# Attention over 16 images: a third buffer for stacked queries and keys, row maxima spread one to a slot, a shorter normalisation chain

## What is computed

```python
xn = (xg - mean) * rsqrt(var + EPS)          # 8 groups of 16 channels, per image
qkv = einsum('oc,bcn->bon', qkv_w, xn) + qkv_b
attn = softmax(einsum('bhdn,bhdm->bhnm', q * scale, k * scale))   # 8 heads, d = 16, n = m = 1024
out = einsum('bhnm,bhdm->bhdn', attn, v)
out = einsum('oc,bcn->bon', proj_w, out) + proj_b + x_in
```

## Time and profile before

| | us |
|---|---|
| median of the 3 runs | 5554.0 (5553.28 to 5566.23) |
| span of the profiled execution | 5548.6 |
| first exponential of image 0, start | 93.0 |
| last exponential of image 15, start | 2121.7 |
| first convolution matmul, start | 2172.2 |
| TensorE busy over the span | 4842.2 (87%) |
| VectorE busy over the span | 3586.2 (65%) |
| ScalarE busy over the span | 2987.7 (54%) |
| GpSimd busy over the span | 1021.9 (18%) |

### The profile page before, as it was taken

One profiled execution on the slowest core, in us unless ns is written; L12 is line 12 of the kernel. 1 busy time (PEld: TensorE's weight loads), 2 busy tenths in 40 slices (PEclk: granted clock), 3 DMA queues, 4 the chain that ended last, 5 costly groups with the idle time before them and its releaser, 6 DMA issues.

```text
span 5548.6 us, 81822 instructions
## 1 busy us (share of the span) xinstructions
PE 4842.2 (87%) x25633; PEld 2616.5 (47%) x25633; DVE 3586.2 (65%) x7699; ACT 2987.7 (54%) x5420; POOL 1021.9 (18%) x1348
## 2 busy tenths in 40 slices
PE   5888888888888886957888888888899999999999
PEld 1222222222222221336777877787755555555554
DVE  6677777777777762555665656555576676766765
ACT  2655565665655653414555555556755455455552
POOL 2212112121222112202333333333210000000000
PEclk7999999999999998979999999999999999999999
DMA  2522222222222211223545454544321111111112
GB/s 84 144 70 81 81 70 70 70 73 78 73 89 82 66 45 38 29 68 106 165 140 163 141 162 147 157 146 129 106 61 45 50 48 45 50 46 47 52 45 75
DMA packets 406297, 477.10 MB, mean 86 GB/s; under 512 B 87640, under 2 KB 249648, under 8 KB 403760
## 3 DMA queue, kind: packets, MB, share of 16 engines
q1 hardware_dynamic: 372128, 424.84, 25.4%
q0 software_dynamic: 20576, 35.55, 2.3%
q10 hardware_dynamic: 13168, 11.48, 0.8%
HBM read 308.54 MB, written 145.57 MB: 82 GB/s over the span
## 4 chain that ended last, share of the span: by engine, by line
PE 33%; DVE 15%; issue 3%; DVEq 3%; ACT 2%; ACTq 0%; SPq 0%; DMA 0%
PE n_ps_f L2153 4%; PE n_ps_f L2146 4%; PE n_ps_xy L1801 3%; PE n_ps_h L1791 3%; PE n_ps_c L2193 2%; PE n_ps_h L2205 2%; PE n_ps_f L2140 2%; PE n_ps_f L1649 2%; PE n_ps_xy L2209 1%; DVEq L2025 1%; DVE n_stats L971 1%; DVE n_xln L983 1%; PE n_ps_f L995 1%; PE n_ps_h L2209 1%; DVE n_down_weights L2024 1%
## 5 line engine op out<-in xcount | busy, mean ns | idle before, releaser
L597 ACT ACTIVATE a_probs<-ps_b 128x512 f32<-128x512 f32 x2048 | 1111.0, 594 | 794.8 <-PE ps_b L693 782.0
L454 DVE TENSOR_REDUCE a_negmax<-ps_a 128x1 f32<-128x1024 f32 x1024 | 1206.1, 1219 | 378.9 <-PE ps_a L637 369.3
L637 PE MATMUL ps_a<-a_k_stack,a_q_stack 96*128 96x512 bf16 x2048 | 634.6, 396 | 178.8 <-DVE a_negmax L454 89.9
L693 PE MATMUL ps_b<-a_q_stack,a_k_stack 99*128 99x512 bf16 x2048 | 673.6, 391 | 68.2 <-ACT a_probs L597 30.9
L1604 ACT ACTIVATE n_hidden<-n_ps_h,n_b 128x128 f32<-128x128 f32 x1472 | 420.2, 374 | 339.1 <-PE n_ps_h L1791 338.3
L706 PE MATMUL ps_o<-a_probs,a_v_ones 128*32 128x512 f32 x4096 | 562.0, 622 | 0.2 <-ACT a_probs L597 0.2
L637 PEld LDWEIGHTS ps_a<-a_k_stack,a_q_stack 96*128 96x128 bf16 x2048 | 146.1, 99 | 732.2 <-DVE a_negmax L454 468.9
L1801 PE MATMUL n_ps_xy<-n_down_weights,n_hidden 128*128 x2944 | 410.7, 284 | 78.9 <-ACT n_xy L1618 72.8
L693 PEld LDWEIGHTS ps_b<-a_q_stack,a_k_stack 99*128 99x128 bf16 x2048 | 196.2, 100 | 487.8 <-ACT a_probs L597 251.5
L1801 PEld LDWEIGHTS n_ps_xy<-n_down_weights,n_hidden 128*128 128x128 f32 x2944 | 369.1, 196 | 117.0 <-issue 112.8
L1791 PE MATMUL n_ps_h<-n_xy,n_up_weights 128*128 128x128 f32 x2944 | 399.8, 279 | 3.6 <-issue 1.8
(11 more groups left out here) (346 smaller groups left out, 7532.8 us busy)
## 6 DMA issues: line engine op xcount, KB each, us to landing
n_up_weights<-in_L_ffn_W_dram SPq DMA_DIRECT2D x368, 256.0 KB, 2.7
n_up_weights<-score_scratch SPq DMA_DIRECT2D x512, 128.0 KB, 2.9
split_scratch<-a_pieces SPq DMA_DIRECT2D x180, 256.0 KB
a_q_stack<-split_scratch SPq DMA_DIRECT2D x128, 192.0 KB, 3.7
a_k_stack<-split_scratch SPq DMA_DIRECT2D x128, 192.0 KB, 4.1
rows_scratch<-n_zero SPq DMA_DIRECT2D x16, 1472.0 KB, 10.5
outs_scratch<-n_xy SPq DMA_DIRECT2D x176, 128.0 KB, 1.9
n_xg<-rows_scratch SPq DMA_DIRECT2D x80, 256.0 KB
```

The lines of the kernel that those rows point to most:

```text
L454: dve.tensor_reduce(negmax[:, b, t:t + 1], bank, axis=AX.X, op=ALU.max, negate=True).then_inc(ring_read, 1)
L597: act.activation(probs[:, m % PROBS, 512 * k:512 * k + 512], ps_b[:, k, :], ACT.Exp).then_inc(b_exp, 1)
L637: last = pe.matmul(bank[:, cols], q_stack[0:KS, h, 128 * t:128 * t + 128], k_stack[0:KS, h, cols], start=True, stop=True)
L693: pe.matmul(ps_b[:, k, :], k_stack[:, h, 128 * t:128 * t + 128], q_stack[:, h, 512 * k:512 * k + 512], start=True, stop=True).then_inc(b_u ...
```

## The change

- A third stack buffer, laid over the part of `u_cols` that images 12 to 15 will fill at the end (`third`). Buffers are taken in turn by group (`stacks`). Results of images 12 and 13 go to DRAM first (`held_dram`) and are loaded when the last image runs (`load_held`).
- Of the six products four are stored instead of six, since two slots repeat (`STORED`); a stack is loaded as three DMAs of 32 rows by four heads for queries and three for keys (`PAIRED`), and TensorE waits once per group for all six.
- Each slot has one R, four slots ahead of where it stood by group (`LEAD`), 32 in 32 slots.
- Order on TensorE: in even slots the first ring unit, S, W, then the other ring units; in odd slots S, then the ring units. W is in every even slot.
- The normalisation chain is shorter (two operations per Newton step instead of three, fewer for the variance and the shift) and is cut into pieces that stand in slots of their own, as are the moments, `norm2` and `turn2`.
- `normed` has the query product in slot 10, the key product in 12, values in 14 (4, 6 and 9 before). Query, key, value and projection products are whole pairs of matmuls, as they were.
- GpSimd does the first shift of the second group before `divide`.

```diff
-        PRODUCTS = ((0, 0), (0, 1), (1, 0), (1, 1), (0, 2), (2, 0))
+        PRODUCTS = ((0, 0), (1, 1), (1, 0), (0, 1), (0, 2), (2, 0))
+        STORED = ((0, 1, 0, 2), (0, 1, 2, 0))
+        PAIRED = ((0, 1, 2), (0, 0, 2))
+        BUFFERS = 3
+        LEAD = 4
+        HOLD = B - 4
+        third = u_cols[:, HOLD:B, :, :].rearrange("p a c h -> p (a c h)").bitcast(BF16).rearrange("p (s j n) -> p s j n", s=2, j=J)
...
-            work = [(0, ("moments",)), (1, ("sums", 0)), (1, ("norm",))]
-            return work + [(4, ("qk", 0)), (6, ("qk", 1)), (9, ("v",))]
+            work = [(0, ("stats", 0, 0)), (1, ("stats", 0, 1)), (2, ("moments", 0)), (3, ("sums", 0))]
+            work += [(4, ("affine", 0, 0)), (6, ("affine", 0, 1)), (8, ("affine", 0, 2)), (9, ("norm",))]
+            return work + [(10, ("qk", 0)), (12, ("qk", 1)), (14, ("v",))]
...
-            return [(2, ("take", 1)), (8, ("recip",)), (29, ("project",)), (30, ("moments2",)),
-                    (31, ("sums", 1)), (32, ("norm2",)), (34, ("turn2",))]
+            work = [(3, ("take", 1)), (8, ("recip",)), (30, ("project",)), (31, ("stats", 1, 0)), (33, ("stats", 1, 1)), (35, ("moments", 1))]
+            work += [(36, ("sums", 1)), (37, ("affine", 1, 0)), (39, ("affine", 1, 1)), (41, ("affine", 1, 2))]
+            work += [(43, ("norm2", 0)), (45, ("norm2", 1))]
+            return work + [(47 + 2 * k, ("turn2", k)) for k in range(4)]
...
-            work = [(3 + n * 26 // QUAD, ("scores", ahead, g, n)) for n in range(QUAD)]
-            return work + [(18, ("shift", ahead, g, 0)), (30, ("shift", ahead, g, 1))]
+            work = [(n, ("scores", ahead, g, n)) for n in range(QUAD)]
+            return work + [(17, ("shift", ahead, g, 0)), (33, ("shift", ahead, g, 1))]
...
+            def load_stacks(i, g):
+                if G * i + g >= BUFFERS:
+                    sp.wait_ge(b_up, (G * i + g - BUFFERS + 1) * (2 * QUAD))
+                for qk, stack in enumerate(stacks(i, g)):
+                    sp.wait_ge(split_stored[qk], (i + 1) * SPLIT)
+                    for n, slot in enumerate(PAIRED[qk]):
+                        sp.dma_start(stack[2 * D * n:2 * D * n + 2 * D, :, :],
+                                     split_dram[qk, J * g:J * g + J, slot:slot + 2, :, :].rearrange("j s d n -> (s d) j n")).then_inc(stacked(i, g)[0], 16)
...
-                    n = run(works, kind, i, n, table)
+                    units_of_slot = [work for work in works if work[0] in RING]
+                    if m % 2:
+                        shifted_scores(i, m)
+                        n = run(units_of_slot, kind, i, n, table)
+                        continue
+                    n = run(units_of_slot[:1], kind, i, n, table)
                     shifted_scores(i, m)
-                    if m % J < HALVES:
-                        if m >= J:
-                            weigh_values(i, m // J - 1, m % J)
-                        elif kind != "first":
-                            weigh_values(i - 1, G * NT - 1, m % J)
+                    if m >= J:
+                        weigh_values(i, m // J - 1, m % J // 2)
+                    elif kind != "first":
+                        weigh_values(i - 1, G * NT - 1, m % J // 2)
+                    n = run(units_of_slot[1:], kind, i, n, table)
```

195 lines of the change are left out of this document (110 added, 85 removed).

## The result

The changed kernel took 5484.5 us (median of 4 runs, 5470.64 to 5493.7), the kernel before 5556.3 on the same chip (5553.28 to 5566.23). The ratio is 0.9868, its 95% interval 0.985 to 0.9886: **72 us or 1.3% faster**. Forecast were 5438 us and 116 us less, with a range of 5315 to 5525. The profiled execution is the fastest of the four, 14 us under the median: 5470.64 us, span 5468.8, which is 79.8 under the span of before.

A forecast was written before the change was run, and what follows sets the result against it. TensorE was taken to bound it, with a floor of 101.3 us an image; 18.7 of waits made 120.0, 7.6 less. Fourteen images gave 106, the prologue 11, the last image lost 1: 116 less, 5438 us, range 5315 to 5525.

The forecast's parts named there:

- the four slots' 0.87: Wait per four slots holding plain scores (R) in the kernel before, 11 us over 52 slots; the new order removes it.
- (a): Query and key product, slots 10 and 12: shifted scores (S) wait for ScalarE's product reading and exponentials, 6.5 us an image.
- (g): One stretch at the lower clock per image: a third of 4 us, 1.3 us.
- Rival C: Clock falls to 1.2 GHz and stays from slot 0 to 16: 16 us more per image, 5663 us; chance 0.07.
- (b): Value product's bank is read as long as that of plain scores (R); the second R behind waits 0.7 us.
- (f): Second halves of shifted scores (S) and turns of maxima: 1.2 us an image.
- (c): VectorE's statistics, chain and normalisation in slots 0 to 9 exceed its free time; TensorE waits about 3.9 us.
- (d): VectorE's work from slot 30 on (projection read, second chain, norm2, turn2) exceeds its free time: 3.0 us an image.
- (e): ScalarE's reading of the sums and copies of values delay exponentials: 2.1 us an image.
- rival D: Stack comes late: slow query and key loads make R in slot 28 wait some 7.5 us, 5545 us; chance 0.07.
- Rival B: Waits hide nearly all, only product waits and a little clock stay: 109.5 us an image, 5291 us; chance 0.16.
- E: Rival that the kernel does not do what it says; dismissed by the order on TensorE, no chance given.

The follow-up runs named there:

- run 3: The changed kernel with the order inside a slot as in the kernel before (all units, S, then W): 5498.1 us, ratio 0.9885 to before.
- run 10: Changed kernel with exponentials before product readings, first chain an image early, products and projection earlier, but the old order inside a slot: 5389.8 us, ratio 0.9685 to before.
- run 12: Changed kernel with exponentials before product readings, early first chain, earlier products, VectorE's work spread evenly, but the old order inside a slot: 5394.3 us, ratio 0.9708 to before.
- run 1: The changed kernel with ScalarE taking a slot's exponentials before reading the query or key product, first piece rounded later: 5482.5 us, ratio 0.9853 to before.
- run 6: The changed kernel with scratch laid out piece by piece: stores of 128 rows, six loads of 16 rows by 4 heads for three: 5483.9 us, ratio 0.9868 to before.

## Why the prediction came out as it did

It was right in sign and range, and 46 us too low in the median; by the two profiles 36 us of the forecast's 116 were missed. That is a balance of larger misses: the thirteen images fell 27 us short and the prologue 16, 5 more were missed behind the attention's images (7 in the part whose code is the same, less 2 won in the last image), and the image without a next one gave back 12. That these 12 stand against the rest is luck: the forecast had this image equal to the others.

**Order of R, S and W.** The pair came at 2.89 us (forecast 2.84), 1.5 us an image more. That "the four slots' 0.87 goes" holds: 0.6 per four slots in run 3, with one R a slot. What the step did not see is that the time so freed is for the most part taken by waits elsewhere in the image: undone, the order costs some 10 to 14 us of the whole (run 3, by ratio and by median, where the intervals overlap), nothing (run 10), or 11 us by median (run 12).

**(a) and (g), the products.** S lost 2.36, 0.82 and 2.38 us, 5.6 with its second halves, against the forecast's 6.5: right in size and place, and run 1 took it away. (g), "one stretch at the lower clock per image", was mis-sized: 1.3 forecast, and 2.8 measured, as R, S, W and the value product from 991 to 998 us took 0.4, 0.5, 0.9 and 1.1 longer. Rival C had the place right and not the size: the dip follows the two waits, but the clock comes back, and the 1.5 us over the forecast are a tenth of its price (16 us an image). Over the span the mean granted clock was 0.949 against 0.952. The Trainium skill, "TensorE: Matmul & The Clock Gate", section on a second failure mode, says that small idle times between groups of matmuls can make the clock swing between its two levels; the trace agrees with the swing at this place, and the rule alone gives no price.

**(b) to (f).** The value product's wait was 0.45 (0.7). (c) came to 3.2 (the waits at the group sum, 1.05 and 0.69, and 1.41 before the product) against 3.9. From slot 30 on, (d) and (e) together lost 5.6 against 5.1. So an image with a next one should have taken 120.0 and took 122.6: 1.5 of it for (g), 1.5 for the pairs, less what (a) to (c) came in under. These terms are read in an image of 121.7 us with a mean clock of 0.97; the other 0.9 of the mean go with images that have more time at 1.2 GHz (0.945 in four of the thirteen).

**The fourteen images** were taken as equal. The one without a next image gained 19.5 us, not 7.6; the thirteen gained 5.5.

**The prologue** was forecast as 11 us less and came 4.9 more; here the step failed, not a size. "Eight at 204 GB/s bring the stacks some 6 us earlier" had the rate of the stores too high: eight of 256 KB, since now both groups go out ahead, moved 143 to 180 GB/s, not 204. And it left out the loads. The first key load of a stack went out 2.7 us earlier (SyncE's queue, before and then changed):

```profile
49.26 0.43 SPq L286 DMA_DIRECT2D a_k_stack<-split_scratch  x1
```

```profile
46.55 1.25 SPq L317 DMA_DIRECT2D a_k_stack<-split_scratch  x3
```

But R now waits for a whole group, 5.5 us from there, where it waited 2.8 for one head. The first R stayed at 52.03. And "four R more are done ahead, which saves waits in image 0" left out what they cost where they stand: in a loop that goes at VectorE's pace and at half clock, these four, from 92.37 on, and slot 0's own R put the first S from 92.38 to 98.00.

**The third buffer.** "This cover is 6 us thick" was the thinnest place of the argument. The way took 38.0 us in run 1, not 32; forecast were 5.1 and 4.5 for stores and loads, and 9.5 and 6.8 came. TensorE took 39.8 us for these slots (976.83 to R of slot 28, the second pair of the row at 1016.24, which starts at 1016.7), not 38, and the waits (a) and the clock (g) are part of that. So 1.8 us were left, and rival D was that near. Rival B would have run into the stacks, as run 1 did: run 1 hides most of the waits at the products, leaves the stacks where they are, and takes 5482.5 us, not 5291. E fell with the trace.

## What to carry to other kernels

Before taking a wait away, follow the next chain that ends at the same place, and price it without the wait: here 7.4 us of waits hid a stack path with 1.8 us to spare, and nearly all of it came back. When a loop gets a cheaper order but other engines and a transfer are close behind, expect the saving back as waits for these; a side chain that is shorter and in pieces, and an even table, were worth more here (8.6 and 9.5 us an image) than the order (1.3). And price all transfers of a prologue up to the first use, the loads behind the stores too, at a rate measured for their size and layout.

## What the chip showed that was not expected

A store whose DRAM side is 8 heads by 16 rows kept the DMA engines at a share of 0.50 and moved 143 to 180 GB/s; the same bytes as 128 rows had 1.05 and 405 GB/s. The Trainium skill, "DMA: Bandwidth & Descriptors", section on why a DMA increments its semaphore by 16, says that the number of engines used is the largest up to 16 that divides the slowest dimension of both sides. A share of 0.50 for 8 and 1.05 for 128 agrees.

Sixteen engines were not enough, though. Loads of 16 rows by 4 heads had a share of 1.08 and moved 141 GB/s, loads of 32 rows by 4 heads 1.04 and 260: busy engines, half the rate. The Trainium skill, "SBUF — State Buffer", section "Door 1: The DMA port swizzle", says that the rate depends on how many of 16 ports the partitions reach, and that four neighbouring partitions share one. By that, 16 rows reach 4 ports and 32 reach 8, a factor of 2 as an estimate; 1.8 was measured. The rates themselves, 141 and 260 GB/s, lie above the limits that the same section gives for 4 and 8 ports, about 109 and 218; several loads were under way at once here, and no run separates them. No run here varied the rows alone: run 6 changed the stores, the size of a load and their number with them.
